# Graph attention over sorted edges: attributes staged by one gather and one store a batch, the chain's links moved one step on, rows weighed 11 steps behind their scores

## What is computed

```python
s = x_l[src] + x_r[dst] + (edge_attr @ W_e.T)         # per edge, 256 wide
alpha = einsum('ehc,hc->eh', leaky_relu(s, 0.2), att)
ex = exp(alpha - segment_max(alpha, dst)[dst])
out = segment_sum(ex / (segment_sum(ex, dst)[dst]) * x_l[src], dst)
```

## Time and profile before

| what | us |
|---|---|
| median of 3 runs | 3,459.81 |
| lowest, highest run | 3,458.88, 3,461.9 |
| profiled execution, span from first to last instruction | 3,452.9 |
| TensorE busy (matmul) | 3,048.3 (88%) |
| VectorE busy | 1,834.2 (53%) |
| ScalarE busy | 1,508.7 (44%) |
| GpSimd busy | 1,189.9 (34%) |

### The profile page before, as it was taken

The page is one execution under the profiler, slowest core; times in us unless marked ns, Lnnn a source line. Parts: engine busy times, 40 slices in busy tenths (PEclk is TensorE's granted clock), DMA queues, the critical chain, the costliest instruction groups (busy, mean ns, idle before and its releaser), DMA issues. The chain is left out here.

```text
span 3452.9 us, 50836 instructions
## 1 busy us (share of the span) xinstructions
PE 3048.3 (88%) x13612; PEld 2420.6 (70%) x13613; DVE 1834.2 (53%) x3643; ACT 1508.7 (44%) x4936; POOL 1189.9 (34%) x1152
## 2 busy tenths in 40 slices
PE   6678888788888888884999999999999999999999
PEld 5456656566565665563778877877787888888898
DVE  5566666666676666676754564374365435111103
ACT  2067666777667676775322322232231212222232
POOL 4556555565555655630310031030021001222210
PEclk9899899999999999997999999999999988999999
DMA  7556655555665655554211011100001032333361
GB/s 217 152 148 148 145 145 141 143 144 141 149 145 145 147 142 150 136 94 124 52 38 37 27 30 31 41 8 1 15 27 50 1 100 84 128 120 119 119 176 38
DMA packets 288628, 345.06 MB, mean 100 GB/s; under 512 B 155176, under 2 KB 213655, under 8 KB 284512
## 3 DMA queue, kind: packets, MB, share of 16 engines
q1 hardware_dynamic: 232813, 174.79, 19.1%
q0 software_dynamic: 53632, 157.89, 17.6%
q10 hardware_dynamic: 2064, 10.81, 1.0%
HBM read 298.03 MB, written 44.37 MB: 99 GB/s over the span
## 5 line engine op out<-in xcount | busy, mean ns | idle before, releaser
L1470 POOL DMA_INDIRECT a_g<-xl_d,a_ix x480 | 468.1, 975 | 311.6 <-issue 116.0
L1504 PE MATMUL b_pM<-b_m,b_oh 128*112 128x281 f32 x1680 | 513.6, 451 | 28.5 <-DVE g_acc L1644 22.5
L1599 ACT ACTIVATE b_m<-a_g,c_pcx 128x64 f32<-128x64 f32 x1856 | 460.4, 334 | 33.6 <-issue 33.6
L1504 PEld LDWEIGHTS b_pM<-b_m,b_oh 128*112 128x112 f32 x1680 | 327.6, 200 | 156.7 <-issue 69.0
L1470 POOL DMA_INDIRECT XS<-xl_d,a_ix x344 | 333.3, 969 | 216.5 <-issue 91.1
L1637 DVE SCALAR_TENSOR_TENSOR a_r<-a_pS,g_attx 128x528 f32<-128x528 f32 x420 | 286.6, 699 | 198.4 <-remote 91.6
L1599 ACT ACTIVATE b_m<-XS,c_pcx 128x64 f32<-128x64 f32 x1424 | 351.5, 333 | 14.3 <-issue 14.2
L2286 ACT ACTIVATE f_hid<-f_pH,f_b 128x256 f32<-128x256 f32 (+3 forms) x360 | 161.9, 451 | 423.0 <-PE f_pH L2180 409.9
L450 PE MATMUL m_pH<-m_h,m_w 128*128 128x313 f32 (+1 forms) x1280 | 342.3, 426 | 4.5 <-DVE m_h L612 4.5
L125 POOL TENSOR_TENSOR m_rstd<-m_ve,m_mhalf 125x5 f32<-125x5 f32 x41 | 48.0, 1170 | 801.5 <-DVE m_ve L111 801.5
L1497 PE MATMUL a_pS<-g_xr,a_lt 128*128 x840 | 237.1, 406 | 97.8 <-ACT a_pS L1581 60.8
(11 more groups left out here) (413 smaller groups left out, 4629.2 us busy)
## 6 DMA issues: line engine op xcount, KB each, us to landing
a_db<-dl_d SPq DMA_DIRECT2D x212, 224.0 KB
f_w<-in_ffn_W1p SPq DMA_DIRECT2D x16, 1024.0 KB
wide_w<-in_ffn_W1p SPq DMA_DIRECT2D x16, 1024.0 KB
m_w<-in_mix_W SPq DMA_DIRECT2D x8, 1024.0 KB
f_w<-in_ffn_W2p SPq DMA_DIRECT2D x8, 1024.0 KB
a_g<-xl_d,a_ix POOLq DMA_INDIRECT x480
a_lt<-eat_d SPq DMA_DIRECT2D x214, 32.0 KB
eat_d<-a_stage SPq DMA_DIRECT2D x15, 448.0 KB
```

What stands on the lines that cost most here:

```text
L1470: p.indirect_dma_start(out=gathered(t)[:, j, :], out_offset=None, in_=xl_d, in_offset=bass.IndirectOffsetOnAxis(ap=IX[:, t // BSTEPS, n:n ...
L1504: ins = pe.matmul(pM[0:WN, h, 0:MW], OH[:, b, j, :], M[:, b, j, :], start=(j == 2 * h), stop=(j == 2 * h + 1))
L1599: ins = a.activation(m[:, j, part], gathered(ts)[:, j, part], ACT.Copy, scale=of[:, first + j, h, 0:1])
```

## The change

* `WEIGH, SUM, ADD` go from 10, 11, 12 to 11, 12, 13: rows are weighed, summed and added one step later. The buffers `M` and `OH` are now indexed by the item's step instead of the current one.
* The row scan of VectorE moves from the end of tau 0 to tau 1, between its one-hot and its reduction. Every link behind it moves one step on (tau 1 to 2, 2 to 3, 3 to 4, 4 to 5, 5 to 6) on all engines.
* The attributes lie in one DRAM array, transposed and plain side by side (16 KB a row). GpSimd gathers 28 such rows once a batch in one DMA, and SP stores them once a batch in one; before, it was 56 rows once a round in two gathers and two stores. SP loads `a_tix` once a batch. The front block does the same for the first 128 rows in one gather and one store.

```diff
-WEIGH, SUM, ADD = 10, 11, 12
+WEIGH, SUM, ADD = 11, 12, 13
...
-                        a.wait_ge(s["i_ea"], 32)
-                        a.dma_start(eat_d[0:128, :], eaT[:, :]).then_inc(s["i_ea_out"], 16)
-                        a.dma_start(ea_d[0:128, :], ea[:, :]).then_inc(s["i_ea_out"], 16)
+                        a.wait_ge(s["i_ea"], 16)
+                        a.dma_start(eab_d[0:128, :], eab[:, :]).then_inc(s["i_ea_out"], 16)
...
-                        p.indirect_dma_start(out=eaT[:, :], out_offset=None, in_=g["eaT"], in_offset=at).then_inc(s["i_ea"], 16)
-                        p.indirect_dma_start(out=ea[:, :], out_offset=None, in_=g["ea"], in_offset=at).then_inc(s["i_ea"], 16)
+                        p.indirect_dma_start(out=eab[:, :], out_offset=None, in_=g["eab"], in_offset=at).then_inc(s["i_ea"], 16)
...
-                TIX = sb("a_tix", [RI, 1], I32)
-                STG = sb("a_stage", [RI, 2, ED * TE])
+                TIX = sb("a_tix", [BI, 1], I32)
+                STG = sb("a_stage", [BI, 2 * ED * TE])
...
                     def attributes_of(base, c, k):
-                        sp.dma_start(LT[WN:128, k, :, :], eat_d[four(base, c), :].rearrange("i (c e) -> c i e", c=ED)).then_inc(s[f"a_eat{k}"], 16)
+                        sp.dma_start(LT[WN:128, k, :, :], eab_d[four(base, c), 0:ED * TE].rearrange("i (c e) -> c i e", c=ED)).then_inc(s[f"a_eat{k}"], 16)
...
-                    def staged(i):
-                        at = RI * i + 2 * RI
-                        return slice(at, at + RI) if isinstance(at, int) else bass.ds(at, RI)
+                    def staged(i, t):
+                        at = RI * i + 2 * RI + BI * (t // BSTEPS)
+                        return slice(at, at + BI) if isinstance(at, int) else bass.ds(at, BI)
 
                     def slot(i, base, t):
-                        if exists(base, t, 0) and t == TILES_AT:
-                            wait(sp, "s_gathered", 32 * i, 0)
-                            sp.dma_start(TIX[:, :], tl_d[staged(i)].unsqueeze(1)).then_inc(s["s_tiles"], 16)
-                        elif exists(base, t, 0) and t == STORE_AT:
-                            sp.wait_ge(s["s_gathered"], 32 * i + 32)
-                            sp.dma_start(eat_d[staged(i), :], STG[:, 0, :]).then_inc(s["s_staged"], 16)
-                            sp.dma_start(ea_d[staged(i), :], STG[:, 1, :]).then_inc(s["s_staged"], 16)
+                        if exists(base, t, 0) and t % BSTEPS == TILES_AT:
+                            wait(sp, "s_gathered", 32 * i, 16 * (t // BSTEPS))
+                            sp.dma_start(TIX[:, :], tl_d[staged(i, t)].unsqueeze(1)).then_inc(s["s_tiles"], 16)
+                        elif exists(base, t, 0) and t % BSTEPS == STORE_AT:
+                            sp.wait_ge(s["s_gathered"], 32 * i + 16 * (t // BSTEPS) + 16)
+                            sp.dma_start(eab_d[staged(i, t), :], STG[:, :]).then_inc(s["s_staged"], 16)
...
-                            sp.dma_start(M[:, t % 2, :, EA0:EA0 + ED], ea_d[four(base, t - WEIGH), :].rearrange("i (e c) -> e i c", c=ED)).then_inc(s[f"b_ea{t % 2}"], 16)
+                            sp.dma_start(M[:, (t - WEIGH) % 2, :, EA0:EA0 + ED], eab_d[four(base, t - WEIGH), ED * TE:].rearrange("i (e c) -> e i c", c=ED)).then_inc(s[f"b_ea{(t - WEIGH) % 2}"], 16)
...
-                        if t == GATHER_AT:
-                            p.wait_ge(s["s_tiles"], 16 * i + 16)
-                            wait(p, "s_staged", 32 * i, 0)
+                        if t % BSTEPS == GATHER_AT:
+                            p.wait_ge(s["s_tiles"], 32 * i + 16 * (t // BSTEPS) + 16)
+                            wait(p, "s_staged", 32 * i, 16 * (t // BSTEPS))
                             p.sem_inc(s["a_seen"], 1)
-                            for n, a in enumerate((g["eaT"], g["ea"])):
-                                p.indirect_dma_start(out=STG[:, n, :], out_offset=None, in_=a,
-                                                     in_offset=bass.IndirectOffsetOnAxis(ap=TIX[:, 0:1], axis=0)).then_inc(s["s_gathered"], 16)
+                            p.indirect_dma_start(out=STG[:, :], out_offset=None, in_=g["eab"],
+                                                 in_offset=bass.IndirectOffsetOnAxis(ap=TIX[:, 0:1], axis=0)).then_inc(s["s_gathered"], 16)
...
                         if tau == 0:
                             wait(pe, "a_alpha", base, t)
                             pe.transpose(pA[0:CP, 0:TE], AX_[:, par, :, :].rearrange("p h i -> p (h i)"), ident[:, :]).then_inc(s["c_turned"], 1)
-                        elif tau == 3:
+                        elif tau == 4:
                             pe.wait_ge(s["c_p"], n)
                             pe.wait_ge(s["c_cl"], n)
                             for d in range(2):
@@ -1526,7 +1521,7 @@
 
...
-                        if tau == 1:
+                        if tau == 2:
                             pe.wait_ge(s["c_rowscan"], n)
...
-                        if tau == 2:
+                        if tau == 3:
                             pe.wait_ge(s["c_diff"], n)
                             pe.matmul(pA[0:1, 0:GH], FB[:, 0, 0:1], by_item(ident[0:CP, 0:CP])[:, :, 0], start=True, stop=True).then_inc(s["c_new"], 1)
-                        elif tau == 4:
+                        elif tau == 5:
                             pe.wait_ge(s["c_fade"], n)
...
-                        if tau == 3:
+                        if tau == 4:
                             a.wait_ge(s["c_back"], n)
                             a.activation(PCX[:, par, :, :, :].rearrange("p i h d -> p d h i"),
                                          pY[0:TE, 256:256 + 2 * CP].rearrange("p (d h i) -> p d h i", d=2, h=GH)[:, :, :, 0:BI], ACT.Copy).then_inc(s["c_pcx"], 1)
                             a.wait_ge(s["c_pcx"], n)
-                        elif tau == 4:
...
                         if exists(base, t, -WEIGH):
                             ts = (t - WEIGH) % RING
-                            of, m = PCX[:, ts // BSTEPS, :, :, :], M[:, t % 2, :, :]
...
-                        if tau == 2:
+                        if tau == 3:
                             a.wait_ge(s["c_diff"], n)
...
-                        if tau == 5:
+                        if tau == 6:
                             v.wait_ge(s["c_scale"], n)
...
-                        if scoring and tau == 5:
+                        if scoring and tau == 6:
...
-                        if scoring and tau != 5:
+                        if scoring and tau != 6:
...
-                        elif tau == 2:
+                        elif tau == 3:
...
-                        elif tau == 3:
+                        elif tau == 4:
...
-                            v.tensor_tensor(OH[:, t % 2, :, :], nodes[:, :].unsqueeze(1).broadcast_to([TE, IG, WN]),
+                            v.tensor_tensor(OH[:, (t - WEIGH) % 2, :, :], nodes[:, :].unsqueeze(1).broadcast_to([TE, IG, WN]),
                                             DLX[:, four(base, t - WEIGH)].unsqueeze(2).broadcast_to([TE, IG, WN]), ALU.is_equal).then_inc(s["b_onehot"], 1)
...
                         if tau == 1:
+                            v.wait_ge(s["c_rows"], n)
+                            for d, way in enumerate((1, -1)):
+                                ins = v.tensor_tensor_scan(ST[0:1, par, d, 0:CP][:, ::way], ANY[0:1, par, d, :, :].rearrange("p h i -> p (h i)")[:, ::way],
+                                                           pY[0:1, d * CP:(d + 1) * CP][:, ::way], LOW, ALU.add, ALU.max)
+                            ins.then_inc(s["c_rowscan"], 1)
+                        elif tau == 2:
                             v.wait_ge(s["c_cols"], n)
                             v.tensor_copy(IN[:, :], pY[0:CP, 240:242]).then_inc(s["c_init"], 1)
                             v.wait_ge(s["c_init"], n)
                             v.sem_inc(s["c_seen"], 1)
...
-                        elif tau == 2:
...
+                        elif tau == 3:
...
-                        elif tau == 3:
+                        elif tau == 4:
...
-                        if tau == 0:
-                            v.wait_ge(s["c_rows"], n)
-                            for d, way in enumerate((1, -1)):
-                                ins = v.tensor_tensor_scan(ST[0:1, par, d, 0:CP][:, ::way], ANY[0:1, par, d, :, :].rearrange("p h i -> p (h i)")[:, ::way],
-                                                           pY[0:1, d * CP:(d + 1) * CP][:, ::way], LOW, ALU.add, ALU.max)
-                            ins.then_inc(s["c_rowscan"], 1)
-                        elif tau == 1:
+                        if tau == 2:
                             v.wait_ge(s["c_rescan"], n)
                             v.tensor_tensor(FB[:, 0, :], FB[:, 0, :], FB[:, 1, :], ALU.max).then_inc(s["c_max"], 1)
...
```

(17 more changed lines are left out.)

## The result

The changed kernel takes 3,598.20 us (median of 4 runs, 3,593.56 to 3,600.46), the kernel before beside it 3,460.86 (4 runs, 3,458.88 to 3,463.84): ratio 1.0391, 95% interval 1.0375 to 1.0408. It is 137 us slower; 3,573 had been predicted. The profiled execution spans 3,598.7 us and took 3,600.46, 1.8 us more. If the kernel before takes 1.8 us beyond its span too, its profiled execution (span 3,452.9 us) was some 4 us faster than the fastest of its timed runs, and the 6.9 us that the prediction puts around the span are mostly that. So the difference between the two profiles, 145.8 us of span, is larger than that of the medians.

A forecast was written before the change was run, and what follows sets the result against it. The prediction took the gathers to bound the kernel, TensorE's answers coming through only after a string's end. 3,459.8 - 30 (link) + 141 (weighing) + 0 (staging) + 2 (tail) = 3,573 us, range 3,405 to 3,710.

The forecast's parts named there:

- Rows weighed 11 steps behind: GpSimd's gathers wait for ScalarE's weighing: four places, 14.4 us a round, less 5 for two fewer strings; +9.4, +141 in all.
- The sum: Whole kernel: 3,459.8 - 30 (link) + 141 (weighing) + 0 (staging) + 2 (tail) = 3,573 us.
- The rows themselves would still land in time: Row gathers of the edge loop: a step takes 6.8 us and gathers are three steps ahead, so no late rows.
- Link moved: VectorE's row scan, tau 0 to tau 1: removes 1.0 us between restart and add, times 30 batches, -30 us.
- The alternative by which TensorE's clock would come back: TensorE's sums: if the moved link closed the idle gap, 1.74 us returns, 52 over 30 batches; sum 3,521, not 3,573.
- Staging: Attributes by one gather and store a batch: taken as 0; at worst +38 us for GpSimd's extra wait for `a_tix`.
- Tail: One step more in the tail of the kernel: 2.2 us, taken as +2.
- The reading of the bound: Edge loop: something tied to the gathers, not the chain, makes a step long; 6.8 us a step, 95.2 a round.
- two natural experiments: Edge loop steps: 6.2 us each early, before any chain or weighing; 4.6 us at the end, after the last gather.
- The expected profile: Edge loop: line 1721's wait gone, GpSimd waiting for weighing in over 100 places, fewer longer strings, round near 103 us.
- the rival of that run, another clock: Unchanged kernel before, reprofiled: TensorE's clock or transfer rate differs, strings alike, mean gather or matmul 8 per cent apart; no chance given.
- the prediction's cycle of strings and restarts: Edge loop: restart, string of gathers, about 1.9 us until TensorE's answers come through, restart; ten strings a round.

## Why the prediction was right, point by point

- **Rows weighed 11 steps behind: +141 us predicted. The mechanism is right; that the size came near is luck, since neither half of it was right.** The prediction took four held places a round at +3.6 us and two pauses fewer. I counted GpSimd's pauses of over 0.6 us between gathers over nine rounds (from the reduction of step 70 to that of step 196): 10.2 a round with 24.7 us before, 10.0 with 34.6 us after, thus +9.9 us with hardly a pause fewer. By what ended them, ScalarE's weighing ends 5.1 pauses a round with 21.6 us, where it ended 0.6 with 1.8 us; TensorE's scores and "remote" end 3.2 with 9.8 us, where they ended 8.4 with 20.3. Of the 26 pauses over 4 us in these rounds the weighing ends 19. So the new wait mostly took the place of old ones: some five places a round, each 4.2 us where a pause was 2.4 on the mean, or +1.8 and not +3.6. The five give 9.2 us in place of the 14.4, the -5 is -0.5, and the other pauses grew by the rest. A further part of the wait had been put at nothing: GpSimd starts 0.95 us after ScalarE's last activation ends (0.94 to 0.96 us in 45 of the 46 such pauses), so at the restart shown it was 5.0 us behind and not 3.2 + 0.9.
- **The sum: +113 us predicted, +137 measured.** The 9.5 us a round of the profiles are the whole change, and the prediction has 9.4 - 2.0 = 7.4 for it. What is missing, 2.1 us a round in the profiles and 24 us in the medians, is about what the link's move was to bring.
- **"The rows themselves would still land in time"** held at 3,461 us: ScalarE waited for rows 11.0 us (2 places) before and 8.9 (2 places) after, in the stretch 106:1350. In the experiments' condition, where a step is 5.5 us, it did not: 58.9 + 9.0 us in 21 places became 83.8 + 68.5 in 66. There the later start of the gathers reaches the scores as late rows, and not through the end of a string. One wait, two ways to lose by it.
- **Link moved: -30 us predicted, some -9 to -12 seen, in the other condition.** In the changed kernel's own profile the wait of line 1721 is gone and lines 1632 and 1639 have it and more, as the prediction had said. The alternative by which TensorE's clock would come back (-52, from the rows of sums at 3.80 and 2.06 us) did not occur: at the restart above TensorE still stands 2.82 us and its eight sums still take 3.74, and over ten rounds its granted clock was 0.89 after and 0.91 before. The rule of the Trainium skill that the prediction named ("TensorE: Matmul & The Clock Gate", "What's actually happening") is not contradicted by that: at this restart the idle time in front of the sums stayed, and so did the slow sums. Over the loop the slow passes shifted: a sum takes 436 ns on the mean instead of 451, a score of line 1485 452 instead of 414 (line 1490). What the link is worth alone where answers are held was not measured.
- **Staging: 0 predicted; 0 beside the rest of the change, -0.5 per cent alone.** The extra load of `a_tix` was no cost. The wait for it fell from 38.0 us to 11.1. The prediction's reason, that a GpSimd held back elsewhere gets to the load later, fits the run with the old staging and the later weighing (13.2 to 6.8 us). In the kernel with the staging alone it fell too, from 13.2 us (8 places) to 6.7 (1 place), less than the 16 us that it is faster. Over the nine rounds above GpSimd's pauses went from 1.7 to 0.1 us a round there (0.9 of the 1.7 were for `a_tix`, 0.7 for the scores), and the round from 75.6 to 74.6 us, 15 us in the loop: nearly every remaining pause is gone, those for the scores too. Why these go is not shown.
- **Tail: +2, measured 2.5.** From the last reduction to VectorE's first instruction behind the loop it is 1,560.91 - 1,527.61 = 33.3 us before and 1,703.79 - 1,667.99 = 35.8 after.
- **The reading of the bound.** "The chain is therefore not what makes a step long; something tied to the gathers is" stands: in the faster condition the link's move gave little, and the one wait of the gathers for ScalarE, taken apart item by item, gave nearly all back. One of its two natural experiments is weaker than it looks: the step of 4.6 us behind the last gather has its like while gathers run (832.54 to 837.15 us, 4.6). And 9.6 of the 22.7 us that it books to TensorE's scores are "remote" in the earlier trace rows, TensorE's by my reading only. The expected profile was nearly met: 99 places for "over 100", a round of 104.7 us for "near 103"; the fewer and longer strings did not come.

## What to carry to other kernels

Delaying a consumer by a step also delays the release of its buffers: look up every producer that waits for that semaphore, and count the distance that is left in steps, not only the time by which the data is needed. Here the distance to `b_weighed` fell from four steps to three, the very step whose scores release the same gathers, and slack became a second condition in series. Where that distance can't be had back, signal by item: three increments and three more waits a step took the ratio of the whole change from 1.025 to 0.998 and 0.999 where the kernel before takes 3,175 us; at 3,461 us it was not tried. The gather and store a batch are worth keeping by themselves (0.995, in the same condition).

## What the runs showed of the hardware that I had not expected

The same kernel took 3,461 us in one condition and 3,175 in the other, and the whole difference is in the edge loop: rounds of 95.2 and 76.7 us, 15 x 18.5 = 277 of 286. Ten rounds of the kernel before at 3,461 us, of the changed kernel at 3,598, and of each at 3,178 and 3,253 (columns as above):

```profile
576.00:1527.00 951.00, 784.78 (x3216) 574.81 (x3215) 648.79 (x1240) 658.70 (x2579) 554.94 (x572) 0.91 0.60 144
```
```profile
622.00:1668.00 1046.00, 809.59 (x3218) 587.96 (x3218) 651.47 (x1242) 655.99 (x2578) 549.36 (x571) 0.89 0.54 130
```
```profile
478.00:1246.00 768.00, 716.70 (x3222) 544.31 (x3221) 654.19 (x1241) 650.27 (x2584) 557.84 (x573) 0.99 0.76 179
```
```profile
502.00:1321.00 819.00, 732.36 (x3224) 548.08 (x3223) 651.27 (x1242) 654.13 (x2585) 554.01 (x575) 0.98 0.73 168
```

VectorE, ScalarE and GpSimd are busy for the same time in all four, within 2 per cent; their instructions do not get slower, and the transfers move as much per busy share (0.60 for 144 GB/s, 0.76 for 179). TensorE's busy time is 68 us longer at 3,461 us, with a granted clock of 0.91 for 0.99, against 183 us by which the ten rounds are longer; so the rival of that run, another clock, holds a part (a sum takes 451 ns on the mean instead of 405), and a gather costs the same (975 and 979 ns). What else differs is how TensorE's answers arrive. One place in the kernel before at 3,178 us, GpSimd in the middle of a string, and VectorE at the same time:

```profile
559.18 0.94 POOL L1470 DMA_INDIRECT XS<-xl_d,a_ix  x1 [0.30 <-issue]
...
561.74 0.95 POOL L1470 DMA_INDIRECT XS<-xl_d,a_ix  x1 [0.30 <-PE a_pS L1491]
```
```profile
559.66 0.66 DVE L1721 TENSOR_TENSOR_SCAN c_state<-c_any,c_pY 1x116 f32<-1x116 f32 x2
...
561.67 0.71 DVE L1637 SCALAR_TENSOR_TENSOR a_r<-a_pS,g_attx 128x528 f32<-128x528 f32 x1 [0.26 <-PE a_pS L1491]
```

The scan of line 1721 does not wait at all, and VectorE waits 0.26 us for TensorE's scores, in the middle of a string. At 3,461 us the same scan stood until 1.9 us behind a string's end. Counted over the nine rounds, from step 70 to step 196: of VectorE's 64 waits of over 1 us for "remote" at 3,461 us 57 end with no gather under way, 53 of them 0.9 to 2.4 us behind a gather's end, and 7 during a gather. At 3,178 us there is no such wait for "remote", and the 28 for TensorE all end during a gather. Accordingly GpSimd's pauses are 1.2 a round there, 1.7 us in all, against 10.2 and 24.7 us: it runs at its own 58 gathers of 1.25 us, 72.5 of the 76.7 us, and the prediction's cycle of strings and restarts exists only where the kernel takes 3,461 us. The changed kernel has 4.2 pauses and 8.8 us a round at 3,253 us. What switches between the conditions, and what holds TensorE's answers back in one of them, these runs don't tell: I could not choose the condition, and no kernel was measured in both beside the two that are compared here. The ten experiments used three chips (11, 14 and 15), and the kernel before took 3,174 to 3,177 us on each; on which chip it took 3,461 is not known, so a difference between chips is not ruled out.
